# Reordering the end of attention: transposes, probability copies, output weights and one raw sum

## The reference, cut to what matters

```python
x = x + xattn(layernorm(x), ctx, Wq, Wkv_expand, Wout)      # softmax(q k^T / 8, causal) v, then @ Wout.T
x = x + bitlinear_ffn(layernorm(x), w_gate, norm_gate, w_down, norm_down)
x = x + moe(layernorm(x), ...)            # router, top 2 of 8 experts, shared expert

def weight_quant(w):                       # in bitlinear, for w_gate and for w_down
    scale = 1.0 / clip(mean(abs(w)), 1e-5)
    return clip(round(w * scale), -1, 1) / scale
```

## Time and profile before

| | us |
|---|---|
| median of 3 runs | 645.24 (644.46 to 646.59) |
| the profiled execution, its own time | 644.07 |
| its span | 642.1 |
| mean granted TensorE clock in it | 0.991 |

### The profile page before, as it was taken

How to read it: one execution, slowest core, us unless ns; L and a number is a source line. 1 busy time by engine, 2 the same in 40 slices (tenths; PEclk the granted TensorE clock), 3 DMA queues, 4 the chain that set the end, 5 groups by cost and what they waited for, 6 DMA issues and landing times.

```text
span 642.1 us, 10562 instructions
## 1 busy us (share of the span) xinstructions
PE 615.5 (96%) x3624; PEld 478.8 (75%) x3625; DVE 528.3 (82%) x899; ACT 423.1 (66%) x558; POOL 146.7 (23%) x145
## 2 busy tenths in 40 slices
PE   8899999998999999969999997999999999999996
PEld 6678888886886444434557886898988989889875
DVE  5898888889687779989998477698897988979687
ACT  4998888889646969885674364557385573846630
POOL 2354445406000333519800300000000000000052
PEclk9999999999999999989999997999999999999999
DMA  8977776764156988727999447595876958769347
GB/s 335 421 303 295 307 294 244 316 266 159 70 220 265 417 362 321 286 120 279 414 384 382 195 157 286 231 372 208 329 278 234 366 211 329 263 251 363 114 162 271
DMA packets 31068, 177.87 MB, mean 277 GB/s; under 512 B 4064, under 2 KB 4064, under 8 KB 14784
## 3 DMA queue, kind: packets, MB, share of 16 engines
q1 hardware_dynamic: 25536, 158.64, 63.6%
q0 software_dynamic: 5504, 18.88, 7.9%
HBM read 154.30 MB, written 23.20 MB: 276 GB/s over the span
## 4 chain that ended last, share of the span: by engine, by line
PE 41%; DVE 22%; ACT 15%; issue 13%; DMA 4%; DVEq 2%; POOL 2%; ACTq 0%; POOLq 0%; SPq 0%
PE BK L306 9%; PE BK L2035 9%; DVE WL L1009 6%; ACT PR L1367 4%; PE BK L2038 3%; ACT RA L1340 3%; PE BK L1882 3%; PE BK L1780 2%; ACT WH L1554 2%; PE BK L312 2%; PE BK L318 2%; PE BK L313 2%; DMA RA<-wbit 2%; DVE BH L891 2%; DMA RX<-wbit 1%
## 5 line engine op out<-in xcount | busy, mean ns | idle before, releaser
L2035 PE MATMUL BK<-EX,WH 128*128 128x320 f32 x512 | 135.9, 347 | 3.6 <-DVE EX L1034 3.2
L2038 PE MATMUL BK<-EX,WL 128*128 128x160 f32 x448 | 106.6, 238 | 0.0
L2035 PEld LDWEIGHTS BK<-EX,WH 128*128 128x128 f32 x512 | 94.0, 191 | 6.1 <-issue 3.4
L1009 DVE TENSOR_TENSOR WL<-RA,WH 128x2048 fp32r<-128x2048 f32 x40 | 89.3, 2287 | 9.7 <-ACT WH L1554 9.5
L2038 PEld LDWEIGHTS BK<-EX,WL 128*128 128x128 f32 x448 | 86.7, 194 | 0.3
L1554 ACT ACTIVATE WH<-RA 128x2048 fp32r<-128x2048 f32 x40 | 73.6, 1910 | 2.4 <-PE BK L1882 2.4
L681 POOL DMA_INDIRECT GA<-rows,SLOT x4 | 4.9, 1228 | 246.2 <-DVE WL L1009 245.3
L649 POOL TENSOR_TENSOR HB<-HB,ND (+2 forms) x28 | 31.1, 1126 | 104.6 <-DVE BH L891 103.8
L1439 ACT ACTIVATE RA<-RA,RT 128x2048 int16<-128x2048 f32 x22 | 44.1, 2014 | 8.2 <-DMA RA<-wbit 5.3
L1009 DVE TENSOR_TENSOR WL<-RC,WH 128x2048 fp32r<-128x2048 f32 x20 | 44.9, 2284 | 0.7 <-ACT WH L1554 0.7
L1836 PE MATMUL BK<-TG,XQ 128*128 128x512 bf16 x192 | 42.4, 379 | 0.1
(11 more groups left out here) (310 smaller groups left out, 1574.5 us busy)
## 6 DMA issues: line engine op xcount, KB each, us to landing
RA<-wbit SPq DMA_DIRECT2D x54, 1024.0 KB, 6.6
RA<-wmoe SPq DMA_DIRECT2D x40, 1024.0 KB, 6.6
RC<-wmoe SPq DMA_DIRECT2D x20, 1024.0 KB, 7.7
rows<-ZERO POOLq DMA_DIRECT2D x40, 256.0 KB, 12.6
XG<-rows SPq DMA_DIRECT2D x10, 512.0 KB, 3.6
rows<-YS SPq DMA_DIRECT2D x9, 512.0 KB, 6.0
RA<-wqk SPq DMA_DIRECT2D x7, 640.0 KB, 7.8
RA<-wo SPq DMA_DIRECT2D x4, 1024.0 KB, 7.8
```

Of the source, the lines that this page charges most:

```text
L1009: e.tensor_tensor(WL[m][:, q * RAW:q * RAW + RAW], RC[j][:, :], WH[m][:, q * RAW:q * RAW + RAW].bitcast(f32), ALU.subtract)\
L2035: mm = e.matmul(bank[GBK[f]][:, 0:2 * R], WH[m][:, at], EX[:, k, :, :].rearrange("p a b -> p (a b)"), start=k == 0, stop=k == KD - 1)
L2038: e.matmul(bank[GBK[f]][:, 0:R], WL[m][:, at], EX[:, k, 0, :], start=False, stop=False)
```

## The change

Four edits. On TensorE `transposes(7)` comes ahead of the wait for wo_p 1 and of part (2, 3) of the output product. On ScalarE `wo_hi(3)` comes behind `probs_hi(7)`, the wait for vp_lo and `wo_hi(2)`. WO_ORDER follows it: `wo_lo(3)` on GpSimd waits for four copies where it waited for three, `wo_lo(2)` on VectorE for three where it waited for four. On VectorE the raw sum of chunk 0 comes behind `probs_lo(7)` and `wo_lo(2)`, where it stood ahead of both.

```diff
-WO_ORDER = (0, 1, 3, 2)
+WO_ORDER = (0, 1, 2, 3)
...
             normalise(NPAIR - 1)
-            absum(1, slice(0, 1), 16 * (NPAIR + 1))
             probs_lo(NPAIR - 1)
             wo_lo(2)
+            absum(1, slice(0, 1), 16 * (NPAIR + 1))
             out_lo(NPAIR - 1)
...
             exponentials(NPAIR - 1)
-            wo_hi(3)
             probs_hi(NPAIR - 1)
             e.wait_ge(s("vp_lo"), NPAIR)
             wo_hi(2)
+            wo_hi(3)
             absum_kept(4, 3, 16 * 7, None)
             absum_kept(3, 2, 16 * (NPAIR + 1), (free_a[4], 6))
             out_hi(NPAIR - 1)
...
             wout(0, 0, (0, 1), True, False)
+            transposes(NPAIR - 1)
             e.wait_ge(s("wo_p"), 1)
             wout(0, 0, (2, 3), False, False)
-            transposes(NPAIR - 1)
             attend(NPAIR - 1, False)
```

## The result

The changed kernel takes 651.68 us (median of 6 runs, 650.62 to 653.0) against 645.48 us before (6 runs). The ratio is 1.0093, 95% interval 1.0077 to 1.0109: slower by 6.2 us, where 650.2, or +5.0, was forecast.

What follows compares the result with a forecast made beforehand. TensorE's order was taken to set the end of attention, with a side path to L1826 having 1.44 us slack. Late wsum +3.4 and half clock +1.6 gave +5.0 us: 645.24 + 5.0 = 650.2, range 647.7 to 651.9.

Steps and rivals of the forecast that it cites:

- The chain: Late wo_hi(3) delays GpSimd's wo_lo(3), chunk 1's load, Abs and wsum; TensorE waits 3.86 us at L1826.
- Forecast shift of L1826: L1826 moves from 166.75 to 170.15, +3.40 us, with the attention's gain of 0.46 us lost entirely.
- the upper bound: 5.4 us for the shift at L1826, if chunk 1's load and NG share the transfer all the way.
- GpSimd's duration: GpSimd's wo_lo(3) takes 4.88 us, not 4.60, beside VectorE's own subtraction into WOL, ending at 162.56.
- The transposes: On TensorE, moved ahead of the second product: second PTH copy ends at 154.01, attention product starts at 154.15, gain 0.46 us.
- The clock behind L1826: After about 3.7 us idle, TensorE's matmuls run at half clock, costing 1.6 us; nothing if the clock holds.
- Rival 1: Late sum, clock holds: same wait at L1826, no drop, +3.4 us, 648.6; chance 0.33.
- NG: 0.5 MB load behind chunk 1: own time 4.5 us, landing at 167.4 or up to 2 us later, before VectorE wants it.
- The moved raw sum: On VectorE, 2.28 us moved behind wo_lo(2): hidden, costs nothing unless OTL slips by over 2 us.
- rival 2: Wait is given back at the transfer at 220.12: not slower, 644.8; chance 0.09 together with the third rival.
- Rival 3: Edit works as meant: attention 0.46 us sooner, load not last, GpSimd's WOL done by 159.2; 0.09 together with the second rival.
- Rival 4: More loss: NG shares the transfer (up to +2 us) or clock stays low for 5 us (2.5); 652 and up; chance 0.06.

Runs made afterwards that it cites:

- weights_back: Changed kernel with ScalarE's copies and WO_ORDER as before, transposes and raw sum still moved: 645.33 us against 644.88 for the kernel before, ratio 1.001.
- no_chunk1_sum: Changed kernel without ScalarE's sum of chunk 1, its column a copy of chunk 0's sum: 645.05 us against 644.88 for the kernel before, ratio 1.0003.
- scalar_only: Kernel before with only ScalarE's fourth output-weight copy moved behind the probabilities and wo_hi(2), and WO_ORDER with it: 652.25 us against 644.88, ratio 1.0116.
- copy3_first: Changed kernel with WOH3 copied ahead of WOH2, both still behind the probabilities: 647.77 us against 644.97 for the kernel before, ratio 1.0036.
- tensor_only: Kernel before with only the transposes moved ahead of part (2, 3): 645.24 us against 644.88, ratio 1.0009.
- vector_both: Changed kernel with WOH3 copied first, VectorE making WOL3 then WOL2, chunk 1 loaded after WOL3: 644.18 us against 645.19 for the kernel before, ratio 0.9983.
- filler: Changed kernel with 15 extra thrown-away matmuls on TensorE ahead of the wait for wsum: 649.89 us against 645.19 for the kernel before, ratio 1.008.
- sum_only: Kernel before with only VectorE's raw sum of chunk 0 moved behind wo_lo(2): 645.0 us against 644.97, ratio 0.9995.

## Why the prediction was right

**The chain.** Copy, GpSimd's WOL3, load of chunk 1, Abs, wsum, L1826: right, step by step. `weights_back` and `no_chunk1_sum` each break one link and the 6 us vanish; `scalar_only` has this link alone and the whole loss. Forecast shift of L1826: 3.40 us; measured 4.23. The difference of 0.83 is 0.90 from the later PTH copy, 0.08 from GpSimd (4.96 for 4.88), and -0.16 from the load: from GpSimd's end to Abs it took 4.82 us, and the forecast had 4.98 (0.03 to the issue and 4.95). The measured shift lies within the forecast's bounds, 3.1 to 5.4, but partly by luck: the upper bound stood for a transfer of chunk 1 that shares with NG, and chunk 1 was not slowed (4.7 us to landing, with NG 0.37 us behind it, against 4.9 before).

**GpSimd's duration.** 4.96 us, so the upper row was the right choice. In all traces here its end lies 4.4 to 4.5 us behind the end of a VectorE subtraction that was under way when it started (as recorded: 144.83 and 149.26 before, 159.32 and 163.83 after), and `copy3_first` shows the same block the other way round. The Trainium skill (SBUF — State Buffer, SBUF: two separate sides) says that the one that starts first holds the shared port pair for its whole instruction; the traces agree (2.29 us of VectorE alone, 5.03 in `copy3_first`). The moved reduction, beside GpSimd's subtraction from 159.24, kept its 2.28 us.

**The transposes: the step that failed.** "It will end at 154.01, a gain of 0.46 us." It ended at 154.91 with the ruler off. The twenty transposes stood in the account at full clock, on the strength of a row at 1.00 beside the 1.60 us hole of the old order. But the move makes a stretch of its own: a hole of 1.89 us, then transposes that wait for VectorE between them, and in the changed kernel the clock went to half at 151.2. The second PTH copy started 0.90 us later than worked out, part (2, 3) ran partly at half clock, and the attention product began at 155.22 with the ruler off and not at 154.15. `tensor_only` shows it alone: +0.60 us at L1826. Where the clock held, in `vector_both`, the second PTH copy started at 152.81 with the ruler off (152.77 was worked out) and the 0.45 us came. The mechanism was right and the clock's price was left out of it. What decides between the two clocks here stays open.

**The clock behind L1826.** Forecast 1.6 us, and nothing if it holds; measured 1.62 (12.63 against 11.01) in the changed kernel and 2.7 in `scalar_only`. `filler` takes the idle away and the price goes. Rival 1, late sum with the clock held, did not come in the two profiled executions, whose idle was 3.59 and 4.01 us; the others have no trace.

**NG.** "167.4 or up to 2 us later": it landed near 169.5 with the ruler off, at the far end, and was hidden only because wsum was later still. The forecast took 4.5 us as NG's own, which it was not: in the earlier trace rows NG was issued while the load of chunk 1 had 1.3 us to go. In the seven traces where it was issued less than 0.5 us before that load landed, or after it, it took 3.5 to 3.7 us. So some 2 us were lost behind chunk 1, and all by NG.

**The rest.** The moved raw sum costs nothing (`sum_only`). Nothing is given back behind 207: rival 2 is out, the shift reached the end whole. Rival 3 needed WOL3 by 159.2; it was done at 163.6 with the ruler off. Rival 4, 652 and up, was not the median, though two of the six executions of the changed kernel took 652.09 and 653.0; its clock price of 2.5 us came in `scalar_only` (2.7), its shared transfer in none.

The sum, in the trace of the changed kernel: 4.23 (late wsum, 0.90 of it from the half clock in the attention) + 0.11 (L1826 itself, from its start to the block of 48 in 0.38 us and not 0.27) + 1.62 = 5.96 us.

## What to carry to other kernels

Before moving a step, follow what it releases on every queue to the place where the engines meet again, and write down that path's slack: here it was 1.44 us, at a matmul of two columns, and the edit made wsum 5.6 us later, while it aimed at two holes worth 3 us. Hand the subtraction that frees a buffer to the quicker engine and take it first, as `vector_both` does. Price a wait of TensorE with the clock behind it, and light work pulled into a hole too: here the waits of 3.2 us and more, in all twelve traces, were each followed by half clock, and six of seven times so were light transposes behind a hole of 1.9 us.

## What the runs showed of the hardware that I had not expected

Work at half clock followed an idle of 3.59 us for 3.5 us and one of 4.01 us for over 5.4 us, so the price of a like wait went from 1.6 to 2.7 us between two executions. Transposes behind a hole of 1.9 us ran at half clock in the changed kernel (twenty in 4.02 us) and at full clock in `vector_both` (3.18 us), from the same order of work on TensorE. A 0.5 MB load issued 0.4 us behind a 1 MB load took 5.6 to 5.8 us to land in four traces, against 3.5 to 3.7 where the 1 MB load had landed or nearly so; the 1 MB load in front took its usual 4.7 to 4.9 us.
